# The first block's expert sum in a gated cross-attention kernel: four products in one VectorE operation, all eight added by GpSimd

## The reference, cut to what matters

```python
# layer 0, "xattn": cosine similarity of projected tokens and context
v = LN(x) @ Wv.T + bv ; t = ctx @ Wt.T + bt
x = x + tanh(g_xattn[0]) * (v @ t.T) / max(|v| |t|, 1e-8)
# layer 0, "ffn": 8 experts, the 2 best of a linear gate, softmax over the two
w, sel = top_k(LN(x) @ gate_w.T, 2) ; w_full = scatter(softmax(w), sel)
x = x + tanh(g_ffn[0]) * sum_e w_full[:, e] * (LN(x) @ expert_w[e].T)
# layer 1 needs, from its own small inputs only, a convolution kernel K (S4D):
K[d, l] = 2 * Re( sum_n dC[d, n] * exp(dt[d] * A[d, n] * l) ),   l = 0..127
```

## Time and profile before

| | us |
|---|---|
| median of 3 runs (1543.04 to 1549.01) | 1544.44 |
| the profiled execution, its own time | 1542.8 |
| its span | 1541.0 |
| first instruction of the next stage (end of `stage_front`) | 219.2 |
| TensorE busy over the span | 1201.0 |
| VectorE busy | 1009.2 |
| ScalarE busy | 684.0 |
| GpSimd busy | 595.8 |

### The profile page before, as it was taken

How to read it: one execution, slowest core, us unless ns; L and a number is a source line. 1 busy time by engine, 2 the same in 40 slices (tenths; PEclk the granted TensorE clock), 3 DMA queues, 4 the chain that set the end, 5 groups by cost and what they waited for, 6 DMA issues and landing times. The chain is left out here.

```text
span 1541.0 us, 30934 instructions
## 1 busy us (share of the span) xinstructions
PE 1201.0 (78%) x10597; PEld 812.1 (53%) x10597; DVE 1009.2 (65%) x3914; ACT 684.0 (44%) x1990; POOL 595.8 (39%) x803
## 2 busy tenths in 40 slices
PE   4777633677566679885699998389999969999997
PEld 3443312334344345554477776136666647777775
DVE  7786539999995279861577776647766544444432
ACT  4442234656665344321245444146666643334332
POOL 4667465888877155520332221224433210000000
PEclk7787665566767779996799999579999989898988
DMA  6301031001000511100000000000000000000001
GB/s 162 87 1 42 1 85 48 15 15 32 25 22 21 158 42 27 29 15 14 1 3 3 3 3 3 1 0 1 2 1 2 1 1 1 0 0 0 0 0 55
DMA packets 63679, 35.54 MB, mean 23 GB/s; under 512 B 23925, under 2 KB 61425, under 8 KB 63539
## 3 DMA queue, kind: packets, MB, share of 16 engines
q1 hardware_dynamic: 62234, 33.45, 8.0%
q10 hardware_dynamic: 1304, 0.33, 0.1%
HBM read 25.21 MB, written 6.42 MB: 21 GB/s over the span
## 5 line engine op out<-in xcount | busy, mean ns | idle before, releaser
L2799 DVE SCALAR_TENSOR_TENSOR k_X<-ps,m_gt,k_X 128x128 f32 (+1 forms) x256 | 72.2, 344 | 122.6 <-PE ps L2698 122.6
L2728 ACT ACTIVATE m_hid<-ps,k_b 128x512 f32<-128x512 f32 x128 | 81.8, 684 | 134.5 <-PE ps L2698 127.7
L2698 PEld LDWEIGHTS ps<-k_w,m_hid 128*128 128x128 f32 x1024 | 123.2, 192 | 26.8 <-issue 17.2
L2689 PE MATMUL ps<-m_xnT,k_w 128*128 128x512 f32 x256 | 127.5, 628 | 1.1 <-DVE m_lg L2744 1.1
L2698 PE MATMUL ps<-k_w,m_hid 128*128 128x128 f32 x1024 | 123.4, 275 | 0.0
L2403 POOL TENSOR_TENSOR l_p<-l_p,l_rsum 128x512 f32<-128x512 f32 x64 | 65.2, 1039 | 141.5 <-DVE l_rsum L2636 141.5
L2204 DVE TENSOR_REDUCE g_top<-ps 128x8 f32<-128x1024 f32 x64 | 75.4, 1219 | 50.6 <-PE ps L2072 50.6
L2515 ACT ACTIVATE l_p<-ps,l_shift 128x128 f32<-128x128 f32 x256 | 91.4, 390 | 21.4 <-DVE l_shift L2581 21.4
L1469 DVE MATCH_REPLACE8 c_left<-c_top,c_left 128x128 f32<-128x128 f32 x384 | 100.7, 273 | 0.0
L2152 ACT ACTIVATE g_pT<-ps 128x1024 f32<-128x1024 f32 x64 | 62.1, 1022 | 85.5 <-PE ps L2088 85.5
L708 PE MATMUL ps<-f_expT,f_xeT 128*128 128x512 f32 x128 | 74.3, 711 | 25.5 <-DVE k_X L1084 24.0
(11 more groups left out here) (521 smaller groups left out, 3254.6 us busy)
## 6 DMA issues: line engine op xcount, KB each, us to landing
v_toep<-kpad SPq DMA_DIRECT2D x4, 1024.0 KB, 10.5
fo_dram<-c_fo SPq DMA_DIRECT2D x32, 128.0 KB, 1.7
v_late<-kpad SPq DMA_DIRECT2D x4, 1024.0 KB, 10.5
d_fo<-fo_dram SPq DMA_DIRECT2D x8, 512.0 KB, 3.6
k_X<-in_x SPq DMA_DIRECT2D x8, 256.0 KB, 3.5
out<-k_X SPq DMA_DIRECT2D x4, 512.0 KB, 5.4
f_cx<-in_ctx SPq DMA_DIRECT2D x4, 384.0 KB, 5.0
c_cx<-in_ctx SPq DMA_DIRECT2D x4, 384.0 KB, 3.9
```

Of the source, the lines that this page charges most:

```text
L2689: pe.matmul(ps[:, 4 * u + q, :], k.w1_3[:, e, 128 * q:128 * q + 128], xnT[:, u], start=True, stop=True).then_inc(s["hid_ps"].sem, 1)
L2698: m = pe.matmul(ps[:, 4 * u + 2 + e % 2, j * S:j * S + S], hid[:, u, q, j * S:j * S + S], k.w2_3[:, e, q, :], start=q == 0, stop=q == 1)
L2728: act.activation(hid[:, u, q, :], ps[:, 4 * u + q, :], ACT.Gelu, bias=k.b1_3[:, 2 * e + q:2 * e + q + 1]).then_inc(s["hid"].sem, 1)
L2799: dve.scalar_tensor_tensor(out=xj[u][j], in0=ps[:, 4 * u + 2 + e % 2, j * S:j * S + S], scalar=gt[:, u, j, e:e + 1], in1=xj[u][j], op0=ALU ...
```

## The change

1. **Experts 0 to 3.** VectorE multiplies the four experts' products by their weights in one 128x512 operation and writes them to `part`, which now has eight slots of 128 for each buffer instead of four. It no longer touches `k.X` here. Before it writes it waits until `gather(b-2)` is complete (`xb_done`).
2. **Gather.** GpSimd adds eight slots in a tree, in place: 512, 256 and 128 wide, then 128 wide into `k.X`. ScalarE's wait for the buffer is now for the whole `gather(b-2)`, not for its first add.
3. **S4D one step up.** `sixteens_a` now stands in step 1, `sixteens_b` in step 2, `sixteens_c` in step 3; the small matmuls in TensorE's step 4 before `experts(b0 + 5)`; the copy to `k2` at the end of ScalarE's step 4; `skip` in GpSimd's step 5 after gather 26, so that SyncE's stores can run beside gathers 27 to 31. `k.vmask` is built at the end of VectorE's step 4.
4. **Norms.** The 16 matmuls of `c_norms` become 8, with a two-column constant `halves` in which each column is one on its half of the partitions; three small memsets make it.

```diff
@@ GpSimd
             def skip():
-                pool.wait_ge(xb_done, B)
+                pool.wait_ge(xb_done, (TURNS - 1) * PAIR + 3)
@@
             def gather(b):
+                p, n = part[:, b % 2], 3 * b
                 pool.wait_ge(scaled, 4 * (b + 1))
-                pool.tensor_tensor(half_sum[:], part[:, b % 2, 0:2], part[:, b % 2, 2:4], ALU.add).then_inc(half_done, 1)
-                pool.wait_ge(half_done, b + 1)
-                pool.tensor_tensor(whole[:], half_sum[:, 0], half_sum[:, 1], ALU.add).then_inc(whole_done, 1)
-                pool.wait_ge(whole_done, b + 1)
-                pool.wait_ge(x_done, 4 * (b + 1))
-                pool.tensor_tensor(k.X[:, b, :], k.X[:, b, :], whole[:], ALU.add).then_inc(xb_done, 1)
+                pool.wait_ge(x_done, b + 1)
+                pool.tensor_tensor(p[:, 0:4], p[:, 0:4], p[:, 4:8], ALU.add).then_inc(half_done, 1)
+                pool.wait_ge(half_done, n + 1)
+                pool.tensor_tensor(p[:, 0:2], p[:, 0:2], p[:, 2:4], ALU.add).then_inc(half_done, 1)
+                pool.wait_ge(half_done, n + 2)
+                pool.tensor_tensor(p[:, 0], p[:, 0], p[:, 1], ALU.add).then_inc(half_done, 1)
+                pool.wait_ge(half_done, n + 3)
+                pool.tensor_tensor(k.X[:, b, :], k.X[:, b, :], p[:, 0], ALU.add).then_inc(xb_done, 1)
@@ steps on GpSimd
+                    if i == 2 and s == 5:
+                        skip()
                 if s == 1:
                     sixteenth()
+                    sixteens_a()
                 if s == 2:
-                    sixteens_a()
+                    sixteens_b()
                 if s == 3:
-                    sixteens_b()
-                if s == 4:
                     sixteens_c()
@@ TensorE, c_norms
-                        for u in range(2):
-                            r = slice(64 * u, 64 * u + 64)
-                            m = pe.matmul(ps[:, 1 + u, i + j:i + j + 1], sq[r, j * S:j * S + S], k.ones[r, 0:1],
-                                          start=True, stop=True)
+                        m = pe.matmul(ps[:, 1, 2 * (i + j):2 * (i + j) + 2], sq[:, j * S:j * S + S], halves[:],
+                                      start=True, stop=True)
@@ ScalarE, experts(b)
                 if b >= 2:
-                    act.wait_ge(half_done, b - 1)
+                    act.wait_ge(xb_done, b - 1)
@@ VectorE, experts(b)
-                for e in range(4):
-                    if e:
-                        dve.wait_ge(x_done, 4 * b + e)
-                    dve.scalar_tensor_tensor(out=k.X[:, b, :], in0=ps[:, 4 + 2 * b % 3, 128 * e:128 * e + 128],
-                                             scalar=wf[:, t % 2, i, e:e + 1], in1=k.X[:, b, :], op0=ALU.mult,
-                                             op1=ALU.add).then_inc(x_done, 1)
+                if b >= 2:
+                    dve.wait_ge(xb_done, b - 1)
+                dve.tensor_tensor(part[:, b % 2, 0:4, :], ps[:, 4 + 2 * b % 3, :].rearrange("p (e c) -> p e c", e=4),
+                                  wf[:, t % 2, i, 0:4].rearrange("p (e o) -> p e o", o=1).broadcast_to([128, 4, 128]),
+                                  ALU.mult).then_inc(x_done, 1)
```

More of the change, by code:

```diff
@@ L267, in stage_front @@
         hit, wf = tmp("hit", [128, PAIR, 2, 8]), tmp("wf", [128, 2, PAIR, 8])
-        part, half_sum, whole = tmp("part", [128, 2, 4, 128]), tmp("half_sum", [128, 2, 128]), tmp("whole", [128, 128])
+        part = tmp("part", [128, 2, 8, 128])
         spare = k.x3[:].rearrange("p c b -> p (c b)")
@@ L290, in stage_front @@
                               "w_done", "den_done", "xp_done", "u_done"))
-        par_done, last_in, cmr_done, cshift_done, kps, k2_done, k2d_done = (once(n) for n in ("par_done", "last_in", "cmr_done", "cshift_done", "kps", "k2_done", "k2d_done"))
+        par_done, halves_zero, halves_done, last_in, cmr_done, cshift_done, kps, k2_done, k2d_done = (once(n) for n in ("par_done", "halves_zero", "halves_done", "last_in", "cmr_done", "cshift_done", "kps", "k2_done", "k2d_done"))
         tmaskf_done, turned1, copied, film_ps, gram_ps, row_done, late_done, bd2T_done, dcoef_done, wup_done = (
@@ L440, in _ @@
             pool.memset(k.ones[:], 1.0).then_inc(consts, 1)
+            pool.memset(halves[:], 0.0).then_inc(halves_zero, 1)
+            pool.wait_ge(halves_zero, 1)
+            for u in range(2):
+                pool.memset(halves[64 * u:64 * u + 64, u:u + 1], 1.0).then_inc(halves_done, 1)
+                pool.wait_ge(halves_done, u + 1)
             pool.iota(iraw[:], pattern=[[1, 8]], base=0, channel_multiplier=0).then_inc(consts, 1)
@@ L758, in _ @@
                     e_turn(s - 1, 1)
+                if s == 4:
+                    pe.wait_ge(copied, 2)
+                    pe.wait_ge(u_done, 1)
+                    pe.wait_ge(xp_done, 1)
+                    for i in range(32):
+                        for g in range(4):
+                            d = 32 * g + i
+                            m = pe.matmul(ps[32 * g:32 * g + NA, 1, NB * i:NB * i + NB], U[:, d, :], XP[:, d, 0:NB],
+                                          start=True, stop=True)
+                    m.then_inc(kps, 1)
                 if main:
@@ L777, in _ @@
                     m.then_inc(gram_ps, 1)
[L778 to L787, removed]
         @block.scalar
@@ L835, in experts @@
                 if b >= 2:
-                    act.wait_ge(half_done, b - 1)
+                    act.wait_ge(xb_done, b - 1)
                 for e in range(4):
-                    act.activation(part[:, b % 2, e, :], ps[:, 4 + (2 * b + 1) % 3, 128 * e:128 * e + 128], ACT.Identity,
+                    act.activation(part[:, b % 2, 4 + e, :], ps[:, 4 + (2 * b + 1) % 3, 128 * e:128 * e + 128], ACT.Identity,
                                    scale=wf[:, t % 2, i, 4 + e:5 + e]).then_inc(scaled, 1)
@@ L886, in _ @@
                                        ACT.Identity).then_inc(exp_done, 1)
-                if s == 5:
-                    act.wait_ge(kps, 1)
-                    for g in range(4):
-                        act.activation(k2[32 * g:32 * g + NA].rearrange("p d b -> p (d b)"), ps[32 * g:32 * g + NA, 1, :],
-                                       ACT.Identity).then_inc(k2_done, 1)
                 if main:
@@ L924, in _ @@
                     experts(b0 + 7)
+                if s == 4:
+                    act.wait_ge(kps, 1)
+                    for g in range(4):
+                        act.activation(k2[32 * g:32 * g + NA].rearrange("p d b -> p (d b)"), ps[32 * g:32 * g + NA, 1, :],
+                                       ACT.Identity).then_inc(k2_done, 1)
         @block.vector
@@ L1014, in c_most @@
                 dve.wait_ge(norms_ps, t + 1)
-                dve.tensor_scalar(inv[:], ps[:, 1:3, 0:2 * G], LEAST, None, ALU.max).then_inc(most_done, 1)
+                dve.tensor_scalar(inv[:], ps[:, 1, 0:4 * G].rearrange("p (c u) -> p u c", u=2), LEAST, None,
+                                  ALU.max).then_inc(most_done, 1)
             def c_add(t, u):
```

13 lines of the change are left out of this document (4 added, 9 removed).

## The result

The changed kernel takes 1563.93 us (median of 4 runs, 1563.23 to 1566.09) against 1543.74 for the kernel before (4 runs, 1542.35 to 1549.01): ratio 1.0124, 95% interval 1.0103 to 1.0146. It is 20.2 us slower. I had forecast 7 more, with a range that ended at 1562. The profiled execution took 1564.27 us with a span of 1562.5 (before: 1542.8 and 1541.0).

A forecast was written before the change was run, and what follows sets the result against it. It took the stage as bound by hand-overs, then by GpSimd's queue: start 56.2 + work 154.5 - 1.0 + waits 14.2 = 223.9, next stage 225.5 instead of 219.2, so +6.3 us and 1550.8 forecast; range 1540 to 1562.

The forecast's parts named there:

- The first add, 1.34 us a gather, 42.9 in all: GpSimd's gathers: the tree's 512-wide add makes each 1.34 us longer, 42.9 us over 32, against 41.2 of room.
- The tail, 8.4 to 1.6 us: Stage end: stores run beside the last five gathers, so of 8.4 us only 1.3 + 0.3 stay.
- Rival 3: Stage end: the stores are not hidden, the tail stays 8 us, 1557; chance 0.05.
- Half of the 3.7 us of norm matmuls goes: TensorE's norms: in step 1 `c_inverse`, and all behind it on GpSimd, starts 1.8 us earlier.
- In steps 2 and 3 it is not on the path: Norm matmuls in steps 2 and 3: their saving is not on the path there.
- Waits that stay on GpSimd: GpSimd's waits after the change, (a), (b) and small ones (c): together 14.2 us.
- Term (a): GpSimd before gather 4, waiting for VectorE's LayerNorm and multiply: 1.5 us in steps 2, 3 and 4, 4.5 in all.
- Term (b): GpSimd before gather 21 in step 4, behind transposes, small matmuls, experts and ScalarE: 6.4 us.
- Cover gone: before, GpSimd could be late without holding VectorE: VectorE, at most two sequences ahead of GpSimd after the change, is held by it, and TensorE waits in turn.
- The sign that I had set: GpSimd waits over 25 us would mean that a chain over the engines binds, not GpSimd's work.
- Rival 2: Port contention beside GpSimd's adds stretches VectorE's eight LayerNorm operations to 8.0 us, 12.7 more over three steps, 1563.5; chance 0.18.
- Rival 1: Added work fits GpSimd's idle time: lighter VectorE makes the 14.2 us of waits vanish, 1536.6; chance 0.15.

The follow-up runs named there:

- the experts' part alone: Kernel before with only VectorE's one multiply, eight slots of `part` and GpSimd's tree of eight: 1577.19 us, ratio 1.0194.
- fillers: Changed kernel plus 128x512 matmuls on TensorE in steps 2 to 4, results overwritten by the transposes: median 1560.02 us, ratio 1.0119 to the kernel before.

## Why the prediction was wrong

- **The first add, 1.34 us a gather, 42.9 in all: right.** 3.08 against 3.09, and GpSimd taken for 153.8 against 153.5. Without the add the stretch is 39.0 shorter. The Trainium skill's rule (GPSIMD Engine Reference, "Engine selection"), to keep element-wise work on VectorE, which I had weighed as speaking against the move, holds here: the experts' part alone cost 28.9 us. The estimate of 1.11 us from the Trainium skill's 2.6 cycles an element (GPSIMD Engine Reference, "Elementwise — side-by-side cycle accounting") was low by 0.15 against the measured 1.26. The adds took 0.45, 0.72 and 1.26 us for 128, 256 and 512 elements, which is 0.27 for each 128 and 0.18 besides.
- **The tail, 8.4 to 1.6 us: right** (1.46), and with it that the stores land beside the experts. Rival 3 is out.
- **"Half of the 3.7 us of norm matmuls goes": wrong,** it was nothing. I halved the time with the number of matmuls. Each record lasts 350 ns in either form, and those of half the height had run two at a time. `c_inverse` came at 53.71 where I had 51.5: 2.2 us of the miss, though in the second profile of the same kernel it came at 56.58. My "In steps 2 and 3 it is not on the path" was wrong too: the norms stand in the chain to gather 5, and half of them left out took 0.64 us off the wait in step 3. The Trainium skill says (TensorEngine Tiling (Array Packing), "Key Properties") that different tiles can load weights and multiply in parallel. The trace agrees for two tiles of 64 rows: two records start every 0.21 us.
- **"Waits that stay on GpSimd", 14.2 us: the step that failed,** 24.3 measured. Term (a) had 1.5 us before gather 4 of each step, measured 1.85. Term (b), 6.4 before gather 21, was 7.74, and 6.57 with fillers. What I left out is the same chain in steps 2 and 3, 3.84 and 2.50 us, 6.3 of the 10.1 missing: behind the LayerNorm come two sets of transposes with the norms and the dots between them, then the experts of sequence 5. At the higher clock it is 11 us and just hidden behind gather 4 and `c_inverse`. In the change it took 15.0 and 13.4, at a mean clock of 0.66 and 0.75. The trace of before had pointed at it, inside the 33.2 us that I took as one sum: from the LayerNorm's start to gather 5 it has 12.4 and 12.5 us at a clock of 0.73, and waits of 1.65 and 4.02 at its end. In step 2, and the end in step 3:

```profile
76.61 0.71 PE L691 MATMUL ps<-k_ident,f_xe 128*128 128x128 f32 x4 [1.31 <-DVE f_xe L1010]
77.25 1.87 PE L664 MATMUL ps<-k_ones,f_v 64*128 64x1 f32 x16
...
126.76 0.72 POOL L566 TENSOR_TENSOR f_half_sum<-f_part 128x256 f32<-128x256 f32 x1 [4.02 <-ACT f_part L838]
```

- **"Cover gone: before, GpSimd could be late without holding VectorE"**: I wrote that and priced it at nothing. VectorE now waits for GpSimd, and TensorE for VectorE. In the changed kernel from 56 to 240:

```profile
PE ps L710 <- DVE f_part L1087: 41.2, 13, 9.9
...
DVE f_part L1087 <- POOL k_X L577: 31.1, 8, 11.5
```

  Before, TensorE waited 24.0 us for VectorE's reading of the experts. It worked 29.1 of 43 us in step 2 instead of 33.1, and the step's granted clock fell from 0.90 to 0.73. In the chain itself the clock was no better before (0.73 in both steps, now 0.66 and 0.75), so the low clock there isn't new, and that the lost cover is what keeps it low is argued from these waits, not tested alone. The fillers, which leave every other instruction in place, show what it costs: they take 8.0 of the 10.3 us by which the stretch missed (184.3 against 174.0). The other 2.3 are the rest of the waits (16.5 against 14.2).
- **The sign that I had set** for the waits, over 25 us, was too far out: at 24.3 a chain over the engines already bound gather 5 of steps 2, 3 and 4.
- **Behind the stage:** 2.65 us in the profile that the forecast did not have, within the 1320.7 to 1328.5 that the same code takes. With 2.2, 10.3 and 2.65 the 15.2 us between +6.3 and +21.5 are complete.
- **Rival 2** gave 1563.5, all but the measured time, and that is luck: its size was wrong. The eight LayerNorm operations took 4.17 us, not 8.0, and the wait that it names, before gather 4, was 1.85, not 5.7. What is left of its mechanism is small: only the first of the eight lasted as long as the 512-wide add beside it (1.28 us, and the second starts at 86.53, when the add ends; before 0.74, beside a 256-wide add of 0.72), and TensorE's chain began 3.2 us after the LayerNorm's start instead of 2.1. A number that fits is no evidence for its mechanism.
- **Rival 1** had it that waits vanish because VectorE is lighter. VectorE's work fell (19.3 us of 43, from 34.0, in step 2), and the waits stayed.

## What to carry to other kernels

When work moves to an engine that others hand over to, ask what the waiting engines lose besides time: a chain on TensorE behind a wait may run at half the clock (0.66 here over the chain, 1.00 with fillers), so take matmul durations at both levels from the trace and put the longer ones into the range. Don't price matmuls by their number; look whether their records overlap. Look at each wait of before by itself, not at the sum: a short wait at the end of a long chain marks the place where the next limit is. And measure a change's parts one by one: here one was worth 11 us and was buried under another that cost 29.

## What was unexpected in the hardware

- More matmuls made the stage faster: 30 fillers took 8.0 us off (184.3 to 176.3). In step 2 the clock on the chain was 1.00 instead of 0.66, and the chain took 11.1 us instead of 15.0.
- Sixteen half-height matmuls (64 rows, one column) took 3.7 us, and so did eight full-height ones with two columns, at 348 and 352 ns a record: every 0.21 us two of the former start, or one of the latter. At the higher clock they took 2.1 and 2.0.
- Beside nearly continuous GpSimd adds the first operation of VectorE's LayerNorm lasted 1277 ns, as long as the 512-wide add that had started just before it (342 is the median of all 32), yet all eight were through in 4.17 us. The other way round, the 512-wide adds averaged 1384 ns against 1268, one of them, beside a 2.28 us VectorE operation, 3.17.
